# A graph network kernel: fifteen of its edge groups gather through TensorE, and the sums over edges are taken in bf16 parts

## The reference

```python
h = jnp.maximum(_layernorm(x), 0.0)
# three times: (segment_sum(h[src], dst) / count) @ Wl.T + b + h @ Wr.T, relu after the first two
x = x + sage3(h)
h = jnp.maximum(_layernorm(x), 0.0)
# GINE
messages = gelu((h[src] + edge_attr) @ We1 + be1) @ We2 + be2
aggregated = segment_sum(messages, dst)
x = x + gelu(((1 + eps) * h + aggregated) @ Wu1 + bu1) @ Wu2 + bu2
```

## Time and profile before

| | before |
|---|---|
| median of 3 runs | 976.62 us |
| lowest, highest | 975.94, 2135.52 us |
| profiled execution (its span) | 981.04 us (979.3 us) |
| PE busy | 879.7 us (90%) |
| DVE busy | 485.6 us (50%) |
| ACT busy | 250.2 us (26%) |
| POOL busy | 383.6 us (39%) |
| HBM traffic | 68 GB/s |

### The profile page before, as it was taken

One profiled execution on the slowest core, in us unless ns is written; L12 is line 12 of the kernel. 1 busy time (PEld: TensorE's weight loads), 2 busy tenths in 40 slices (PEclk: granted clock), 3 DMA queues, 4 the chain that ended last, 5 costly groups with the idle time before them and its releaser, 6 DMA issues.

```text
span 979.3 us, 20510 instructions
## 1 busy us (share of the span) xinstructions
PE 879.7 (90%) x7824; PEld 653.8 (67%) x7824; DVE 485.6 (50%) x1882; ACT 250.2 (26%) x433; POOL 383.6 (39%) x411
## 2 busy tenths in 40 slices
PE   2977999999999999999809999999999899899883
PEld 1733555555554455555609999998988888898882
DVE  6589999995111121121348545445445545445431
ACT  2576677773110110011102111111111111111111
POOL 2000000000000001111277777777777777777771
PEclk9969999999999999999959999999999999999987
DMA  4200001102000000000174444444434444434321
GB/s 137 63 2 12 3 13 13 12 13 65 1 1 1 1 1 11 11 10 17 49 170 108 134 120 137 133 113 130 138 102 134 117 117 130 117 107 130 106 63 32
DMA packets 46635, 67.90 MB, mean 69 GB/s; under 512 B 15396, under 2 KB 25349, under 8 KB 46402
## 3 DMA queue, kind: packets, MB, share of 16 engines
q1 hardware_dynamic: 34626, 42.11, 15.5%
q0 software_dynamic: 11904, 24.40, 9.8%
HBM read 63.18 MB, written 3.30 MB: 68 GB/s over the span
## 4 chain that ended last, share of the span: by engine, by line
PE 64%; DVE 12%; POOL 10%; issue 7%; DMA 3%; ACT 2%; SPq 0%; ACTq 0%; POOLq 0%; DVEq 0%
PE f_ps L1132 26%; PE f_ps L1183 11%; POOL f_adj L545 10%; PE f_ps L1237 8%; PE f_ps L1168 7%; DVE f_region L594 2%; PE f_ps L1017 2%; DVE f_region L592 2%; PE f_ps L1010 2%; PE f_ps L1107 2%; DVE f_region L598 2%; DVE f_region L596 2%; DMA f_adj<-in_dst_next 1%; DMA inv<-f_rstd 1%; PE f_ps L1069 1%
## 5 line engine op out<-in xcount | busy, mean ns | idle before, releaser
L545 POOL DMA_INDIRECT f_adj<-table,f_table_idx x372 | 359.4, 966 | 113.4 <-issue 112.8
L1132 PE MATMUL f_ps<-f_adj,f_parts 125*128 125x500 fp8e4 (+1 forms) x1575 | 331.5, 352 | 0.1
L1132 PEld LDWEIGHTS f_ps<-f_adj,f_parts 125*128 125x128 bf16 x1575 | 143.5, 97 | 130.0 <-issue 11.1
L1183 PE MATMUL f_ps<-f_parts 125*128 125x128 bf16 x3300 | 200.0, 220 | 0.0
L1183 PEld LDWEIGHTS f_ps<-f_parts 125*128 125x128 bf16 x3300 | 193.2, 98 | 6.4 <-issue 4.4
L530 POOL TENSOR_TENSOR f_rest<-f_region,f_parts 125x512 f32<-125x512 f32 (+1 forms) x7 | 7.3, 1050 | 461.5 <-ACT f_parts L975 461.5
L1237 PE MATMUL f_ps<-f_adj 128*128 128x94 f32 (+20 forms) x984 | 131.9, 280 | 30.3 <-ACT f_adj L997 28.2
L870 DVE TENSOR_TENSOR f_adj<-f_ps,f_adj 128x512 f32<-128x512 f32 x93 | 64.1, 689 | 186.1 <-issue 116.0
L1237 PEld LDWEIGHTS f_ps<-f_adj 128*128 128x128 f32 x984 | 120.9, 195 | 37.9 <-issue 34.3
L997 ACT ACTIVATE f_adj<-f_adj 128x512 f32<-128x512 f32 x93 | 58.4, 630 | 336.8 <-DVE f_adj L870 332.5
L887 ACT CAST f_adj<-f_ps 128x500 f32 x213 | 126.1, 592 | 56.7 <-PE f_ps L1017 40.8
(11 more groups left out here) (135 smaller groups left out, 478.7 us busy)
## 6 DMA issues: line engine op xcount, KB each, us to landing
f_region<-in_edge_attr_T SPq DMA_DIRECT2D x104, 256.0 KB
f_adj<-table,f_table_idx POOLq DMA_INDIRECT x372
f_parts<-in_src_row SPq DMA_DIRECT2D x11, 256.0 KB, 3.7
f_adj<-inv SPq DMA_DIRECT2D x1, 1562.5 KB, 7.7
table<-f_region SPq DMA_DIRECT2D x6, 250.0 KB
out<-f_xT SPq DMA_DIRECT2D x6, 250.0 KB, 2.5
f_rcntT<-inv SPq DMA_DIRECT2D x5, 250.0 KB, 3.8
f_xT<-in_xT SPq DMA_DIRECT2D x1, 812.5 KB, 6.0
```

The source lines that it names most:

```text
L545: pool.indirect_dma_start(out=rows[:, r % RW, j * D:(j + 1) * D], out_offset=None, in_=table, in_offset=bass.IndirectOffsetOnAxis(ap=table ...
L1132: ins = pe.matmul(ps[:, dense_ps(i):dense_ps(i) + width(c)], parts[0:NP, (l % 2) * 3 + p, b, :], adj[0:NP, b, lo:hi].bitcast(F8), start=b ...
L1183: ins = pe.matmul(z_ps(g, j), select[0:NP, u % SELECT, j * P:(j + 1) * P], parts[0:NP, 3 + p, b, :], start=b == 0 and j == 0 and p == 0, s ...
```

## The change

Four things change.

1. **Groups and picks.** The last tile (five real edges) is a group by itself, so there are 105 groups: 103 of four tiles, one of three, one of one. Fifteen groups are picked instead of eleven: 3, 9, 16, 23, 29, 36, 43, 50, 56, 63, 70, 76, 83, 90, 97 (before: 8, 17, ..., 98). A slot ahead of a picked group now has four or five blocks of selections (eight or nine in slots 0 to 2) instead of three.
2. **Sums over edges in bf16.** Except in the last group, ACT takes the Gelu twice, to bf16 (`msg_part(g, 0)`) and to f32; DVE subtracts (`leave_high`), ACT copies to bf16, DVE subtracts again (`leave_mid`). PE multiplies three bf16 parts with bf16 one-hots: 12 bf16 matmuls for a group with one piece instead of 4 in f32.
3. **Order on DVE.** In slot g: leave_high(g-1), window one-hots of g+2, leave_mid(g-1), the add of group g, selections.
4. **The check in pieces.** The operations of `check_input` are spread over slots 0 to 10 of the edge stage, PE's L1218 moves to slot 12, and the reduction over the counts moves into slot 221 (`CALM = GB + 8`) of the first stage.

```diff
-        self.FG = -(-self.FT // self.FTG)
+        self.FG = -(-(self.FT - 1) // self.FTG) + 1
-        self.PERIOD = 9
-        self.picked = list(range(self.PERIOD - 1, self.FG - self.FTG, self.PERIOD))
+        self.SHARES = 15
+        reach = self.FG - 2 * self.FTG
+        self.picked = [self.FTG - 1 + i * (reach - self.FTG + 1) // (self.SHARES - 1) for i in range(self.SHARES)]
...
-        onehot, o = carve(flat, o, (OH, T, W), F32)
+        onehot, o = carve(flat, o, (OH * T, W), BF16)
+        onehot_end, o = carve(flat, o, (T, W), F32)
+        msg_parts, o = carve(flat, o, (MP * 3, T * D), BF16)
...
+            def check_repeats():
+                dve.memset(flag[:, :], 0.0).then_inc(cleared, 1)
+                dve.wait_ge(cleared, 1)
+                dve.wait_ge(count_in[0], 16 * ((NC + 1) // 2))
+                dve.wait_ge(count_in[1], 16 * (NC // 2))
+                dve.tensor_reduce(flag[0:NB, 2:3], c25[0:NB, :], AX.X, ALU.max).then_inc(repeats, 1)
...
+                if slot == CALM:
+                    check_repeats()
...
+            def leave_high(g):
+                dve.wait_ge(msg_ready, g + 1)
+                dve.tensor_tensor(msg_left(g), msg[:, g % MS, 0:s.tiles(g) * D], msg_part(g, 0), ALU.subtract
+                                  ).then_inc(left_ready, 1)
+
+            def leave_mid(g):
+                dve.wait_ge(mid_ready, g + 1)
+                dve.tensor_tensor(msg_part(g, 2), msg_left(g), msg_part(g, 1), ALU.subtract).then_inc(low_ready, 1)
...
-            check_input()
             for g in range(END):
...
+                if 1 <= g < G:
+                    leave_high(g - 1)
+                if g + OH_AHEAD < G:
+                    window_onehots(g + OH_AHEAD)
+                if 1 <= g < G:
+                    leave_mid(g - 1)
                 if g < G:
-                    if g + OH_AHEAD < G:
-                        window_onehots(g + OH_AHEAD)
...
+                if g == 0:
+                    check_tiles()
+                if g == 1:
+                    check_steps()
+                if g == 2:
+                    check_windows()
+                if g == 4:
+                    join_checks()
...
             for g in range(END):
+                if 1 <= g < G:
+                    act.wait_ge(left_ready, g)
+                    act.copy(msg_part(g - 1, 1), msg_left(g - 1)).then_inc(mid_ready, 1)
...
+                    if g < G - 1:
+                        act.activation(msg_part(g, 0), summands, ACT.Gelu)
                     act.activation(msg[:, g % MS, 0:w], summands, ACT.Gelu).then_inc(msg_ready, 1)
...
-                    pe.wait_ge(msg_ready, g + 1)
+                    if g < G - 1:
+                        pe.wait_ge(low_ready, g + 1)
+                    else:
+                        pe.wait_ge(msg_ready, g + 1)
```

122 lines of the change are left out of this document (76 added, 46 removed).

## The result

The changed kernel takes 1015.13 us (median of 4 runs, 1014.56 to 1017.12) against 977.16 us of the kernel before beside it: 1.039 times as long, 95% interval 1.0374 to 1.0406. It is slower, and 28.6 us above the predicted 986.5. The profiled execution has a span of 1012.7 us, 23.5 above the sum's 989.2. One run of the kernel before, of 2135.52 us, lies far outside the others and is left out of the ratio.

A forecast was written before the change was run, and what follows sets the result against it. PE was taken to bound the kernel, POOL its last 150 us. Slots 0 to 3 end at 523.9, slots 4 to 97 add 425.3, then 26.6, 0.7 and 13.3: span 989.2, median 986.5 (+1.0%), range 962 to 1003.

The forecast's parts named there:

- the median is 2.7 less: Last step, from span to median: the median lies 2.7 us below the profiled span, so 989.2 becomes 986.5.
- POOL, -20.3 us, pitch 1.271: Gathers on POOL: 16 fewer, 356 in all, one per 1.271 us, saving 20.3 us.
- PE's start: PE's first edge-stage selection: 23.4 us earlier without the check ahead, 3.1 later for the moved reduction, so 495.9.
- Head, slots 0 to 3: First edge slots: 28.0 us, ending at 523.9, with 3.0 for DVE's lateness and one cold start of 1.3.
- Selections, 55.8 ns: PE's selection matmuls in the edge stage: 1200 more at 55.8 ns each, +67 us.
- Parts, 42 ns a record, 0.50 us a group: PE's bf16 sums over edges: 12 records of 42 ns, 0.50 us a group, -58 us for all aggregates.
- Slot, 4.10 and 4.77: PE's work per edge slot: 4.10 us with four blocks of selections, 4.77 with five; PE leads the 3.9 us chain.
- Picked wait, 15 times 2.15: Picked groups: PE stands 2.15 us behind the chain of Gelus and parts, 15 times.
- Node waits, 9.4: Node updates in the 3.9 us chain: 9.4 us of waits for five chunks; a picked slot hides the mix.
- Tail, 3.9, 3.9, 3.9, 4.75, 5.2, 5.0, then 0.7: Groups 98 to 104 at the chain's pace: 26.6 us, then 0.7 for last add, one Gelu and hop.
- The first rival: Edge stage: waits are covered and POOL binds to the end; median 959.5, chance 0.08, with half-way cases 0.15.
- POOL slows down: Rival on POOL's gathers: at +0.15 us each, span 1015; takes over from a pitch of about 1.35; chance 0.04.

The follow-up runs named there:

- e8_lag_calm: Changed kernel, all gathers on, with PE's sum over edges one slot later and the check's reduction five build slots later: 971.82 us.
- n8_base: Changed kernel without the gathers behind the first six groups by rows, otherwise unaltered: 1014.05 us.
- n3_f32: Changed kernel without the later gathers, with f32 sums instead of parts, fifteen picked groups: 1015.61 us.
- n7_before: Kernel before, without the gathers behind the first six groups by rows: 941.73 us.
- e9_f32_sums: Changed kernel, all gathers on, with f32 sums instead of parts, fifteen picked groups: 987.20 us.
- n2_lag: Changed kernel without the later gathers, with PE's sum over edges one slot later: 971.92 us.
- n4_busy: Changed kernel without the later gathers, with 56 small extra matmuls on PE ahead of the sum in picked and last slots: 1011.49 us.
- n5_order: Changed kernel without the later gathers, with DVE's node sum and node add moved behind the low part: 1005.38 us.

## Why the prediction was wrong

The mechanism was right: PE stands behind the chain of parts at each picked group, 1.94 us against 2.15, and the slot with it takes 3.58 against 3.57. The step that failed is what a stand costs and what lies in the chain. The sum charged a stand with its own length and nothing behind it, and it left a piece of the check out of the chain and underpriced the node steps in picked slots. The runs show a lower clock behind some stands (1.6 us each, 6.5 in the steady part and 2.0 in the tail), 1.6 us for slot 4 and 1.9 more for node steps. Beside that, smaller terms were too low: PE's slots by 4.5 us in all, the head by 4.2. That PE's first selection came within 0.8 us of its forecast is luck. The span was short by 23.5 us, at these places:

| stretch | predicted end or length | measured | off |
|---|---|---|---|
| to the end of slot 3 | 523.9 | 528.1 | +4.2 |
| slots 4 to 97 | 425.3 | 440.7 | +15.4 |
| sums 97 to 104 | 27.2 | 31.9 | +4.7 |
| last sum to the end | 13.3 | 12.5 | -0.8 |

The other 5.1 of the 28.6 us come from the last step, "the median is 2.7 less" than the span. The profiled execution of the kernel before (981.04 us) stood 4.4 us above the median, that of the changed kernel (1014.83) stands at it, so here the median is 2.4 us more than the span. That step took one execution's place among the others for a property of the kernel.

- **POOL, -20.3 us, pitch 1.271.** Wrong in size, without effect here: 969.7 - 490.6, less 15.1 us of waits for DVE, over 355 is 1.307 us. Where POOL binds (e8_lag_calm) it is the term that decides.
- **PE's start.** Predicted 495.9, measured 495.13, by two deviations that cancel. This execution was ready for L1178 at 251.91, 2.1 us earlier than the kernel before (254.05), which has nothing to do with the change: traces without the moved reduction have 250.14 to 254.05 there. And the reduction cost 4.7 us here, not 3.1, since the clock fell behind PE's stand of 2.90; in n8_base it stays up, and the reduction costs 3.0 (last section). So the 3.1 was right but for the clock.
- **Head, slots 0 to 3.** The step "landed some 2.6 later" failed: group 0's add waits for its gather until 501.00 (498.6 predicted), so the first sum starts at 506.53 instead of 504, and PE stands 3.23 us. Slots 1 to 3 take 21.1 us from sum to sum instead of 19.4; the clock is 0.82 from 490 to 520, and the sum had one cold stretch of 1.3 us.
- **Selections, 55.8 ns.** Right: 48 take 2.68 us. From sum 3 to sum 97, with f32 sums in both, n3_f32 (fifteen picks, 4200 selections in the stretch) takes 438.8 us and n7_before (eleven, 3156) 381.0: 57.7 us for 1044 more, 55 ns each. The Trainium skill's 81 ns a pair ("TensorE: Matmul & The Clock Gate", Back-to-back issue gap) would give 85 us, an estimate, and the traces don't agree with it.
- **Parts, 42 ns a record, 0.50 us a group.** Right (12 in 0.52). But "-58 us" was too much. A slot with f32 sums takes 4.52 us in e9_f32_sums and 4.15 with parts, and from sum 3 to sum 97 it is 438.8 us (n3_f32) against 389.8 (n2_lag, whose stretch has 60 selections or 3.3 us fewer): -46 for 94 sums, so some -50 for all of them (an estimate). PE's work thus grew by some 17 us (67 less 50), not 9. The slots were summed from the parts' own price, so this doesn't enter the 986.5.
- **Slot, 4.10 and 4.77.** 4.15 and 4.83: +0.05 to +0.06 in 80 slots, +4.5 us. Sums in two pieces add 0.5 more than was charged, and PE's L1292, which had no term, 0.2.
- **Picked wait, 15 times 2.15.** 1.94 to 1.97 in ten of them, right. What failed is that nothing was charged behind it. The clock falls after some of the stands: in the stretch of slots 4 to 97 four slots of the changed kernel are 1.6 us longer than the same ones in n4_busy or n5_order (behind groups 36, 50, 63 and 70), 6.5 us; in the tail 7.25 against 5.28, 2.0 us.
- **Slot 4, 4.77.** This failed too: it takes 6.45. PE is cold in it (0.74), but with the clock at 1.00 in n4_busy it still takes 6.06. DVE is busy for the whole slot: a piece of the check that the change puts there, 1.91 us, stands ahead of leave_high(3). So the check in pieces costs 1.2 us here and the clock 0.4. The row of the changed kernel:

```profile
529.13 1.91 DVE L873 TENSOR_REDUCE f_flag<-f_adj 1x1 f32<-1x1704 f32 x1
```

- **Node waits, 9.4; "a picked slot hides the mix".** The size is nearly right: with the clock's part taken out they come to some 11.3 us (worked out slot by slot from the trace), and a chunk in slots of four selections costs 2.7 (2.65 predicted). The hiding failed. DVE's node_sum stands ahead of leave_high and waits for that mix, so the mix is inside the chain: slot 36 takes 5.95 where the sum has 3.57 + 1.47 = 5.04. With the order changed it takes 3.58, so the mix could have been hidden whole. Another chunk's up step falls into picked slot 70: a stand of 3.94 us, and 6.42 for the slot where 3.57 + 0.84 is 4.41; that one stays in n5_order. Two other chunks could gain 0.7 each by the order (5.94 and 5.37 against 5.63 and 4.99). Node waits (1.9), clock behind picked groups (6.5), slot 4 (1.6) and slot rate, pieces and L1292 (5.2) are 15.2 of the 15.4 us.
- **Tail, 3.9, 3.9, 3.9, 4.75, 5.2, 5.0, then 0.7.** Measured 3.89, 3.89, 3.88, 4.78, 7.25, 6.04, 2.20. The first four are right. The fifth needs two things at once: it is 5.28 with the clock at 0.98 (n4_busy), and 4.38 with the clock at 0.50 where DVE's node_sum stands behind leave_mid (n5_order), so it is a mix at the lower clock inside the chain of parts. The last group's two f32 sums come 1.5 us later than "one Gelu and a hop", since PE does a chunk's down matmul of 2.01 us ahead of them at the lower clock (0.84 at the higher).

The tail of the changed kernel, PE only; the node matmuls of 500 columns take 1.87 to 2.02 us for two instead of 1.00:

```profile
984.74 1.12 PE L1316 MATMUL f_ps<-f_adj 128*128 128x95 bf16 x12 [3.16 <-DVE f_adj L814]
...
986.21 1.87 PE L1271 MATMUL f_ps<-f_adj,f_We 128*128 128x500 f32 x2
...
991.99 0.82 PE L1316 MATMUL f_ps<-f_adj 128*128 128x84 bf16 x12 [2.84 <-DVE f_adj L814]
992.60 2.02 PE L1279 MATMUL f_ps<-f_rcntT,f_Wu 128*128 128x500 f32 x2
998.03 0.58 PE L1316 MATMUL f_ps<-f_adj 128*128 128x54 bf16 x9 [3.41 <-DVE f_adj L814]
998.42 2.01 PE L1283 MATMUL f_ps<-f_hT,f_Wu 128*128 128x500 f32 x2
1000.23 0.47 PE L1316 MATMUL f_ps<-f_adj 128*128 128x32 f32 x2
```

Of the rivals, the chain did not set every slot here (3.88 against 4.15), but does at eleven picks. POOL does not slow enough to bind the changed kernel. The first rival (the waits covered, 959.5) is what e8_lag_calm builds, and it gives 971.82; POOL's pitch, 17 us more over its gathers, is enough for that. "POOL slows down" had the right sign, +0.036 to +0.048 us a gather, and a threshold (1.35) that was never reached. How much of the 28.6 us is clock in an average run stays open to some 5 us, since the falls vary: the runs of n8_base lie between 1013.73 and 1022.47.

## What to carry to other kernels

Cost a new dependency as the stand it makes and what follows the stand: here 1.94 us of standing was followed by up to 1.6 us at the lower clock. When a chain between engines gets longer by half a slot, first move its consumer one slot later: nearly the same instructions in that order took 971.82 instead of 1015.13 us, some 3 us of it by a moved reduction. And in a loop of steps on an in-order engine, a step that waits for another engine belongs behind the steps that this engine is waiting for (8.7 us for an order of four lines).
